# A hybrid transformer block on one core: the half-head exchange is issued first on SyncE, and GpSimd adds before it normalises

## What is computed

```
x = x + attn_a(layernorm(x))
x = x + ffn(layernorm(x))        # the stack, first time
x = x + attn_b(layernorm(x))
x = x + ffn(layernorm(x))        # the stack, second time
```

```
q, k, v = split(shift_tokens(x) @ Wqkv)          # 16 heads of 64
q = l2norm(q) * q_scale ; k = l2norm(k) * k_scale
q = q * cos * scale + rotate_half(q) * sin * scale
k = k * cos / scale + rotate_half(k) * sin / scale
attn = softmax(mask(8 * q k^T))                  # windows of 32 tokens, the one before and its own
x = concat(attn @ v) @ Wo + x
x = ffn_layer(shift_tokens(x)) + x               # layer norm, gated, gelu, 2 matmuls
```

## Time and profile before

| | us |
|---|---|
| three runs | 4369.92, 4377.39, 4368.14 |
| median of them | 4369.92 |
| the profiled execution | 4373.69 |
| its span, first to last instruction | 4372.0 |

### The profile page before, as it was taken

How to read it: one execution, slowest core, us unless ns; L and a number is a source line. 1 busy time by engine, 2 the same in 40 slices (tenths; PEclk the granted TensorE clock), 3 DMA queues, 4 the chain that set the end, 5 groups by cost and what they waited for, 6 DMA issues and landing times. The chain is left out here.

```text
span 4372.0 us, 111762 instructions
## 1 busy us (share of the span) xinstructions
PE 4078.6 (93%) x43089; PEld 2415.8 (55%) x43089; DVE 3362.0 (77%) x4981; ACT 3109.2 (71%) x7032; POOL 1797.4 (41%) x1071
## 2 busy tenths in 40 slices
PE   7997999999999999999967589999999999999998
PEld 3443555555555555555536545555555555555554
DVE  5774888888888888888735478888888888888885
ACT  3555777777777777777762267777777777777776
POOL 3112444444444444444404534444444444444442
PEclk7997999999999999999986599999999999999999
DMA  2212444444443444444300044444444444444342
GB/s 43 31 21 72 96 110 101 106 95 103 104 104 93 112 103 96 106 98 104 80 10 3 3 111 107 103 94 106 108 96 109 99 105 96 103 103 107 93 100 49
DMA packets 232516, 380.70 MB, mean 87 GB/s; under 512 B 59365, under 2 KB 122337, under 8 KB 231689
## 3 DMA queue, kind: packets, MB, share of 16 engines
q1 hardware_dynamic: 231560, 372.20, 36.7%
q10 hardware_dynamic: 384, 0.79, 0.1%
HBM read 39.22 MB, written 1.05 MB: 9 GB/s over the span
## 5 line engine op out<-in xcount | busy, mean ns | idle before, releaser
L835 POOL TENSOR_TENSOR b_prob<-b_prob,b_rinv 128x768 f32<-128x768 f32 x384 | 564.2, 1469 | 1797.0 <-DVE b_rinv L1276 1797.0
L841 POOL TENSOR_TENSOR b_prc<-b_prc,b_sws 128x1024 f32<-128x1024 f32 x384 | 906.7, 2361 | 70.8 <-DMA b_sws<-b_prs 70.6
L1138 ACT ACTIVATE b_prob<-ps,b_nmx 128x96 f32<-128x96 f32 x3072 | 748.9, 362 | 0.0
L1211 DVE SCALAR_TENSOR_TENSOR b_prc<-ps,b_qks,b_rot 128x512 f32<-128x512 f32 x768 | 570.6, 743 | 11.8 <-ACT b_sq L1099 11.5
L1213 DVE SCALAR_TENSOR_TENSOR b_prs<-ps,b_qks,b_rot 128x512 f32<-128x512 f32 x768 | 569.5, 742 | 0.0
L1257 DVE TENSOR_TENSOR b_prc<-b_prc,ps 128x512 f32<-128x512 f32 x384 | 263.5, 686 | 384.9 <-PE ps L942 305.4
L1074 ACT ACTIVATE b_pT<-ps 128x512 f32<-128x512 f32 x724 | 434.8, 601 | 129.8 <-PE ps L879 127.9
L879 PEld LDWEIGHTS ps<-ident,b_prob 128*128 128x128 f32 x3072 | 381.5, 141 | 219.8 <-ACT b_pT L1074 121.3
L879 PE MATMUL ps<-ident,b_prob 128*128 128x128 f32 x3072 | 461.4, 273 | 5.9 <-ACT b_pT L1074 5.8
L982 PE MATMUL ps<-b_wqkv,b_xs 128*128 128x256 f32 x1536 | 434.1, 405 | 2.2 <-DVE b_prs L1213 2.2
L1119 ACT ACTIVATE b_oT<-ps 128x512 f32<-128x512 f32 x384 | 226.8, 591 | 293.7 <-PE ps L899 293.7
(11 more groups left out here) (293 smaller groups left out, 7294.5 us busy)
## 6 DMA issues: line engine op xcount, KB each, us to landing
b_sws<-b_prs SPq DMA_DIRECT2D x1536, 128.0 KB
b_vs<-b_va SPq DMA_DIRECT2D x384, 256.0 KB, 3.8
b_wqkv<-in_L_ffn_Wqkv SPq DMA_DIRECT2D x96, 192.0 KB, 3.5
b_xs<-y SPq DMA_DIRECT2D x126, 128.0 KB, 2.3
b_wo<-in_L_ffn_Wo SPq DMA_DIRECT2D x96, 64.0 KB, 3.2
b_xs<-y SPq DMA_DIRECT2D x42, 127.8 KB, 2.3
b_rot<-in_rot SPq DMA_DIRECT2D x2, 2048.0 KB, 7.9
b_w<-in_L_ffn_W SPq DMA_DIRECT2D x24, 170.5 KB
```

What stands on the lines that cost most here:

```text
L835: pool.tensor_tensor(prob[:, r, :, P - KEYS:P], prob[:, r, :, P - KEYS:P], rinv[:, r % 2, :].rearrange("p (b a) -> p b a", a=1).broadcast_ ...
L841: pool.tensor_tensor(prc[:, r, :, :], prc[:, r, :, :], sws[:, r % 2, :, :], ALU.add)\
L1138: g = act.activation(prob[:, kb, i, P - KEYS:P], wide[0][:, e * CH + m * KEYS:e * CH + (m + 1) * KEYS], ACT.Exp, bias=nmx[:, kb % 2, i:i + 1])
L1211: dve.scalar_tensor_tensor(out=prc[:, r, i, :], in0=bank[i][:, :], scalar=scale, in1=rot[:, 2 * i, t], op0=ALU.mult, op1=ALU.mult)
```

## The change

On SyncE the exchange moves up in the slot: it now stands behind the shift of a finished chunk and ahead of the `vs` copies and of all weight loads. Its second wait is no longer for the add of unit j - 1 but for the landing of the exchange of unit j - 1. On GpSimd the add of unit j - 1 now comes ahead of the normalisation of unit j - 3 in a slot. No instruction is added or removed on any engine but for the wait that changes.

```diff
@@ SyncE, slot
                         for to, frm in shifted(chunk(e)):
                             sp.dma_start(to, frm).then_inc(S["fin_done"], 16)
+                    if a:
+                        U, r = um(a)
+                        sp.wait_ge(S["pk_done"], ONE + U + 1)
+                        if b:
+                            sp.wait_ge(S["swap_ld"], ONE + 64 * (um(b)[0] + 1))
+                        for h in range(4):
+                            o = h ^ 1
+                            sp.dma_start(sws[32 * o:32 * o + 32, r % 2, :, :], prs[32 * h:32 * h + 32, r % 2, :, :])\
+                                .then_inc(S["swap_ld"], 16)
                     if b:
                         U, r = um(b)
                         if r % 2:
...
                         for dst, src in ffw[5 * (j - HALF):5 * (j - HALF) + 5]:
                             sp.dma_start(dst, src).then_inc(S["ffw_ld"], 16)
-                    if a:
-                        U, r = um(a)
-                        sp.wait_ge(S["pk_done"], ONE + U + 1)
-                        if b:
-                            sp.wait_ge(S["add_done"], ONE + um(b)[0] + 1)
-                        for h in range(4):
-                            o = h ^ 1
-                            sp.dma_start(sws[32 * o:32 * o + 32, r % 2, :, :], prs[32 * h:32 * h + 32, r % 2, :, :])\
-                                .then_inc(S["swap_ld"], 16)
@@ GpSimd, slot
                     v, u = unit(1), unit(3)
+                    if v:
+                        U, r = um(v)
+                        pool.wait_ge(S["swap_ld"], ONE + 64 * (U + 1))
+                        pool.tensor_tensor(prc[:, r, :, :], prc[:, r, :, :], sws[:, r % 2, :, :], ALU.add)\
+                            .then_inc(S["add_done"], 1)
                     if u:
                         U, r = um(u)
                         pool.wait_ge(S["rinv_done"], ONE + U + 1)
                         pool.tensor_tensor(prob[:, r, :, P - KEYS:P], prob[:, r, :, P - KEYS:P],
                                            rinv[:, r % 2, :].rearrange("p (b a) -> p b a", a=1).broadcast_to([P, NB, KEYS]),
                                            ALU.mult).then_inc(S["pn_done"], 1)
-                    if v:
-                        U, r = um(v)
-                        pool.wait_ge(S["swap_ld"], ONE + 64 * (U + 1))
-                        pool.tensor_tensor(prc[:, r, :, :], prc[:, r, :, :], sws[:, r % 2, :, :], ALU.add)\
-                            .then_inc(S["add_done"], 1)
```

## The result

| | before | changed |
|---|---|---|
| median, four runs each, us | 4369.6 | 4593.72 |
| lowest to highest | 4368.14 to 4377.39 | 4588.29 to 4604.72 |
| span of the profiled execution | 4372.0 | 4593.0 |
| TensorE busy, us | 4078.6 | 4136.8 |

The change makes the kernel slower by 5.1%: the ratio is 1.0513, with a 95% interval of 1.0493 to 1.0532. Forecast were 4493 us and at most 4565. The change is slower, as forecast, but by nearly twice as much. The span grew by 221 us where the sum had 123.

What follows compares the result with a forecast made beforehand. TensorE, busy 97.9% of the steady stretches, was taken as the bound. 4373.69 + 168 (waits for copies) - 45 (earlier adds) = 4496.7 us, 4493 on the median; forecast's own range 4430 to 4552, 8 in 10 4425 to 4565.

Steps and rivals of the forecast that it cites:

- The waits for the copies, 168 us: TensorE ahead of the value matmuls: copies land 7.3 us behind k's last product, 96 waits, 168 us in 12 layers.
- The 3.9 of every slot: Landing of the second value copy: 3.9 us behind its issue in the median, used for every slot.
- The gain of earlier adds, 45 us: TensorE's waits behind VectorE: adds no longer late and `rsp` faster save 45 us, with 15 and 60 as ends.
- its 117 us: VectorE's `rsp` excess over 740 ns; by the two-sides rule alone all would return wherever GpSimd is idle, some 70 us lower.
- The clock falls in the waits: Rival, chance 0.07: TensorE's clock drops in each of 24 new 3 us waits, 84 us more, 4577 us.
- Weight loads … : nothing: SyncE's weight loads go out at most some us later and are wanted a layer later: no cost.
- The copies did not come in time: Rival, chance 0.08: value copies land in time for TensorE's value matmuls, only the gains are left, 4325 us.
- The landings kept their median: Rival, chance 0.04: value copies in even slots land as late as the longest seen, 293 us of waits, 4618 us.
- The normalisation was not late: Rival, chance 0.04: GpSimd's normalisation comes 0.7 us late for the transposes in 96 places, 67 us more, 4560 us.

Runs made afterwards that it cites:

- the long waits: The changed kernel with the copies behind the exchange only in slots 0, 8, 16 and 24, ahead of it in other even slots; 4515.39 us, ratio 1.0317.
- the short slots alone: The changed kernel with the copies behind the exchange only in slots 4, 12, 20 and 28, ahead of it in other even slots; 4368.55 us, ratio 0.9994.

## Why the prediction was right or wrong

**The waits for the copies, 168 us: right in the sum, in part by luck.** 168.2 were measured, in 94 of 96 places. The path from k's last product to the landing was 7.19 us in slot 8, forecast 7.3. The agreement of the sum hides errors that cancel. From the end of the scores to the first value matmul, TensorE lost, by the starts of lines 968 and 899 and averaged over the layers, 2.3 us in slot 1 (in the ten layers that have this wait) and 2.7 in slot 9 (forecast 2.15 and 3.1), but 2.8 in slot 17 and 3.6 in slot 25. The distances from k's last product to these matmuls do repeat in the second half of a layer, as forecast: in the kernel before 5.4 and 4.5 us on average behind slots 0 and 8, 5.2 and 4.4 behind slots 16 and 24. What does not repeat is the landing: 3.8 us on average for the second copy of slot 8, but 4.5 and 4.6 in slots 16 and 24, and 5.5 in the example of slot 24 (1893.74 to 1899.28), where weight loads follow the copies. The 3.9 of every slot was the wrong step here, and the shorter wait in slot 9 paid for it. Whether the weight loads delay the landing was not tried.

**The gain of earlier adds, 45 us: the size was right, though it was a choice between 15 and 60.** 46 and 43 us, and the rows behind it came as said: the exchange 0.1 us behind the product, no waits for the add, `rsp` at 744 ns. Some two thirds to three quarters come from GpSimd's order alone. How the gain splits between the earlier adds and the faster `rsp` no run shows. The rule of the Trainium skill, "SBUF — State Buffer", section "SBUF: two separate sides", that a VectorE instruction with two SBUF inputs and a GpSimd one exclude each other, agrees with the medians (1114 to 744 ns). But its 117 us did not come back, not even to VectorE. The two lines of `rsp` took 257.4 us before and 191.5 now, 66 less, and another VectorE instruction with both inputs in SBUF, in the feed-forward part, became slow instead. Before, then now:

```profile
L1268 DVE SCALAR_TENSOR_TENSOR cen<-cen,b_lng,sqr x44: 739/742/744, 577.9 to 4262.5; 128x512 f32<-128x512 f32 x44
L1268 DVE SCALAR_TENSOR_TENSOR cen<-cen,b_lng,sqr x44: 741/2138/2886, 577.3 to 4483.1; 128x512 f32<-128x512 f32 x44
```

That is 55 us more, and VectorE's busy time hardly moves (3362.0 to 3358.8). With GpSimd's new order alone the median of this line is 2111 ns, with the new wait alone 742: the earlier add moved the collision more than it ended it.

**"The clock falls in the waits", 0.07: the step that failed.** I gave the forecast a clock of 1.00 because the longest wait before had kept it (the 2.1 us are the weight loader's; by the row itself the matmuls stood for 3.60 - 1.75 = 1.85), and wrote myself that the new waits of 3 us were longer than any seen; nothing in the trace then spoke for 1.00 at 3 us, and the 0.65 between two blocks spoke against. As a rival it had the price about right: 84 us, against 60 by the medians of the long waits, 73 by TensorE's busy time and 81 by the clock records. But it came about otherwise than described, in 38 places of some 2 us each and not in 24 of 3.5. Its time, 4577 against 4593.72, was near too, but the stated range ended at 4565, below it. What was wrong is that the sum of the forecast had nothing for it, and its chance of 0.07. The Trainium skill, "TensorE: Matmul & The Clock Gate", section "HAM oscillation — how this bites in real kernels", describes matmuls that run slow behind every wait for a DMA. The traces agree for the long waits (0.52 behind 4.44 us, and 28 of the 29 of 2.5 us or more); not behind every one of the shorter ones.

**"Weight loads … : nothing": the second step that failed, by omission.** The list of what the copies are moved past and what stands behind them had the weights and not the shift of line 762. Its reader, the mean matmul, comes soon behind it. It cost 33 us, of which 20.6 are idle time of TensorE ahead of that matmul.

**The other rivals.** The copies did not come in time. The landings kept their median, 3.9 us. The normalisation was not late in the change, where no wait of TensorE for it is in the list, but it was in the kernel with the copies in the midst, with an exchange about 2 us later: the mechanism of that rival is real, and the margin is no more than these 2 us.

With both steps filled in from the runs the sum is 4373.7 + 168 - 45 + 73 + 21 = 4590.7 us, or 4587 on the median: 7 us under the measured. The 73 and the 21 are read from the result, so this shows that the terms are complete and not that they could have been forecast.

## What to carry to other kernels

When a transfer moves behind another's wait in a queue, write down every transfer behind it up to the next wait with the time that its reader leaves, not only the one whose line moved; here the reordering gains 1% with the copies in front and loses 5% with them behind. A wait of TensorE that is longer than any in the trace can have two prices, its length and the slower matmuls behind it: where the trace does not reach, put the second into the sum, or give it far more than a chance of 0.07 and let the range reach it. An instruction order on a helper engine (GpSimd's add ahead of a wait that has nothing to do with it) can be worth 0.7% by itself.

The best version here is the change with the copies of the values in front of the exchange: 4325 us, 1% under the kernel before.

## What the chip showed beyond that

- In the stacks of the changed kernel a stretch at 1.2 GHz follows none of TensorE's 78 gaps of 0.5 to 1.5 us, 4 of 14 up to 2.0 us, 6 of 13 up to 2.5 and 28 of 29 that are longer. The shortest gap with one behind it is 1.87 us, ahead of the value matmul at 508.14 us. The window there:

```profile
508.00:514.00 6.00, 5.86 (x43) 4.10 (x44) 2.27 (x3) 2.88 (x10) 1.54 (x2) 0.72 0.39 90
```

- With the copies behind in the short slots alone, one wait of 2.07 us was followed by such a stretch (0.76 over the 7 us from 2572), and another of 2.04 us by none. So the length of a wait alone does not decide, and what does is left open.
- The low clock comes late in the wait and stays behind it: the window up to 1898, with 3.2 of the 4.44 us, shows 1.00, and the next, with the last 1.3 us of the wait and 5.7 us of work, 0.52. What is lost is in the work.
- Matmuls that compute nothing of use, 1.80 us of them in each long wait, made the kernel 51 us faster, though still 3.8% slower than the kernel before.
- A VectorE instruction of 742 ns with both inputs in SBUF took 2138 ns in the median once a GpSimd add of 2.37 us was moved to the same moment (L1268 above), while another that the add left fell from 1114 to 744.
- Two copies of 256 KB in the midst of four exchange DMAs cost 121 us over the same copies ahead of them (4446.37 against 4325.42), though TensorE's waits for the copies were 28 us.
